# A decoder layer on one core: scores two batches behind, heads inside the loop, two single last batches

## The reference, cut to what matters

```
# 1. attention, 16 heads of 8 channels
q_in = x @ Wq.T + b ; Q = [q_in, conv3(q_in)] @ qproj.T + b      (K the same way, V = x @ Wv.T + b)
tau   = sigmoid(conv1(gelu(dwconv3(x))))                         one value per head and query
delta = sigmoid(conv1(gelu(dwconv3(x))))                         one value per head and key
scores = (Q K^T / sqrt(8)) * tau + delta ; attn = softmax(scores) ; out = attn V @ out_w.T + b
# 2. cross part (mLSTM form), 4 heads of 32 channels, q from the result, k and v from ctx
i, f gates ; log_D = lower triangle of (cumulated log f differences + i) ; D = exp(log_D - rowmax)
C = (q k^T / sqrt(32)) * D ; h = C / max(|sum C|, exp(-rowmax)) @ v ; head norm, times (1 + ln_weight)
# 3. linear with x and weight rounded to a 6 bit grid in blocks of 32, plus bias
```

## Time and profile before

| | us |
|---|---|
| runs | 257.17, 258.87, 253.48 |
| median | 257.17 |
| profiled execution, its own time | 257.06 |
| its span, first to last instruction | 255.2 |
| TensorE busy | 197.6 |
| VectorE busy | 157.1 |
| ScalarE busy | 122.8 |
| GpSimd busy | 130.3 |

### The profile page before, as it was taken

The page is one execution under the profiler, slowest core; times in us unless marked ns, Lnnn a source line. Parts: engine busy times, 40 slices in busy tenths (PEclk is TensorE's granted clock), DMA queues, the critical chain, the costliest instruction groups (busy, mean ns, idle before and its releaser), DMA issues. The chain is left out here.

```text
span 255.2 us, 6255 instructions
## 1 busy us (share of the span) xinstructions
PE 197.6 (77%) x2279; PEld 135.3 (53%) x2279; DVE 157.1 (62%) x383; ACT 122.8 (48%) x333; POOL 130.3 (51%) x246
## 2 busy tenths in 40 slices
...
PEclk9999869899999999799985999989999999555555
...
GB/s 182 147 185 1 3 0 1 1 0 3 3 0 3 85 0 3 85 0 4 3 85 3 0 105 3 0 106 1 6 100 6 3 103 23 2 85 0 21 21 21
DMA packets 11454, 8.94 MB, mean 35 GB/s; under 512 B 2745, under 2 KB 10401, under 8 KB 11425
## 3 DMA queue, kind: packets, MB, share of 16 engines
...
HBM read 7.47 MB, written 1.08 MB: 34 GB/s over the span
## 5 line engine op out<-in xcount | busy, mean ns | idle before, releaser
L1005 DVE TENSOR_REDUCE nm<-score 128x8 f32<-128x1024 f32 x32 | 39.0, 1222 | 24.1 <-PE score L604 24.0
L501 ACT ACTIVATE u<-score 128x1024 f32<-128x1024 f32 x32 | 32.6, 1018 | 27.7 <-PE score L616 27.7
L604 PE MATMUL score<-km,qf 32*128 32x512 f32 x128 | 36.2, 662 | 5.0 <-ACT u L501 3.0
L610 PE MATMUL score<-qm,kf 32*128 32x512 f32 x128 | 37.0, 652 | 0.0
L813 PE MATMUL bankPV<-u,vz 128*32 128x128 f32 x512 | 18.6, 290 | 6.5 <-ACT u L501 6.5
L286 POOL TENSOR_SCALAR qm<-qf,mcol 128x512 f32<-128x512 f32 x16 | 11.7, 749 | 23.0 <-DVE qf L993 16.9
L616 PEld LDWEIGHTS score<-nmT,sel 32*128 32x128 bf16 x256 | 10.9, 95 | 18.0 <-issue 18.0
L863 PE MATMUL bankY<-ctm,xt 128*128 128x33 f32 x128 | 18.4, 303 | 2.0 <-ACT y1s L515 0.6
L813 PEld LDWEIGHTS bankPV<-u,vz 128*32 128x32 f32 x512 | 14.0, 114 | 10.4 <-ACT u L501 8.6
L863 PEld LDWEIGHTS bankY<-ctm,xt 128*128 128x128 f32 x128 | 17.6, 220 | 3.2 <-DVE xt L1070 2.0
L813 PE MATMUL bankPV<-u,ez 128*32 128x128 f32 x512 | 18.7, 291 | 0.0
...
## 6 DMA issues: line engine op xcount, KB each, us to landing
...
```

Source lines behind the costliest of these rows:

```text
L501: nc.scalar.activation(prob[:, i % 2, k:k + 2, :].rearrange("p k s -> p (k s)"), sc[:, 512 * k:512 * (k + 2)], ACT.Exp, scale=SQ_SCALE).th ...
L604: ins = mm(sc[:, 512 * k:512 * (k + 1)], qf[r, n, :], km[r, n % (2 * CB)].rearrange("p j s -> p (j s)"), start=True, stop=True)
L610: mm(sc[:, 512 * k:512 * (k + 1)], kf[r, n, :], qm[r, n % (2 * CB)].rearrange("p j s -> p (j s)"), start=True, stop=False)
L1005: nc.vector.tensor_reduce(nm[:, i % 2, J * k:J * (k + 2)], sc[:, 512 * k:512 * (k + 2)].rearrange("p (h s) -> p h s", s=S), AX_X, ALU.max, ...
```

## The change

- `GR` replaces the eight pairs by nine groups: seven pairs, then batches 14 and 15 alone. Every step of the rest takes its width from it.
- Scores: `v1.i` and `v2.i` now hold a(i) and b(i-2). Two new steps `aa.0`, `aa.1` hold a(0), a(1) alone, `bb.14`, `bb.15` hold b(14), b(15) alone. `nm`, `nmx` and `nmT` get three buffers instead of two.
- Heads: `u` has two chunks instead of four, so the middle tap of chunk 2 or 3 waits until `tau` or `del` two chunks before is done. In the lists the taps 6 and 7, their gelus, `tau.2`, `tau.3`, `del.3` and their tanh stand inside the loop. For them ScalarE loads the gelu set again (`gelu.1`) and then the exp set again (`exp.1`). exp(delta) and its transpose are made by chunk. `diag` and the unused convolution step are gone. ctx chunks 2 and 3 are loaded once `cT.0`, `cT.1` have freed their buffers.
- Groups 7 and 8 (`BY_ROWS`): `dec` no longer reads the spread gates. A new TensorE step `ld` writes a bf16 mask into bank P and adds each gate row by a matmul with one column of the identity, repeated over all partitions; `dec` takes four exponentials with the other gate as bias. `spread` is not issued for them, nor `dm`.
- The step `hl` (GpSimd) multiplies by (1 + ln_weight) right after `hs`; `z2` and the centring inside `qa` are VectorE's. `hc` and `zc` are gone, `zb` follows `qa`, and `z2`, `z2c`, `z2b`, `z3` share one buffer `z`.
- `y1s` has five buffers instead of three. In `y1` the residual's matmul comes first.

```diff
+GR = ((0, 2), (2, 2), (4, 2), (6, 2), (8, 2), (10, 2), (12, 2), (14, 1), (15, 1))
+BY_ROWS = (7, 8)
+YR = 5
-TAU_BANK = ("S2", "S3", "PV", "PV")
+TAU_BANK = ("S2", "P", "P", "P")
+DEL_BANK = ("Y", "P", "P", "P")
 PE_ORDER = """
+    tx.0 ab.0 hw.0 mT.0 mT.1 wT.0 tx.1 del.0 tx.2 wT.1 tau.0 K.0 del.1 Q.0 Q.1 tx.3 del.2 aa.0 Q.2 gw.0 aa.1 tau.1 cg.0 nmT.0 ow.0 v1.2 nmT.1 K.1 edT.0
+    v2.2 edT.1 K.2 v1.3 V.0 edT.2 rc.0 v2.3 nmT.2 cT.0 pv.0 cm.0 v1.4 cm.1 pv.1 nmT.3 v2.4 V.1 y1.0 v1.5 nmT.4 tau.2 v2.5 gF.0 pv.2 v1.6 nmT.5 pv.3 tau.3
+    yT.0 del.3 MT.0 K.3 v2.6 edT.3 y1.1 V.2 v1.7 nmT.6 V.3 pv.4 qk.0 gF.1 V.4 v2.7 hst.0 v1.8 MT.1 pv.5 nmT.7 v2.8 cT.1 yT.1 v1.9 cT.2 pv.6 dT.0 v2.9
...
+    v1.15 nmT.14 pv.12 v2.15 y1.5 cm.7 pv.13 nmT.15 bb.14 dT.3 cm.8 y1.6 gF.5 qk.4 ffn.3 MT.5 pv.14 yT.5 bb.15 gF.6 hst.4 qk.5 MT.6 y1.7 yT.6 pv.15 hst.5
+    yT.7 qk.6 y1.8 gF.7 dT.4 ld.7 ffn.4 gF.8 qk.7 hst.6 dT.5 ld.8 ffn.5 MT.7 hst.7 yT.8 MT.8 qk.8 dT.6 ffn.6 hst.8 dT.7 ffn.7 dT.8 ffn.8
 DVE_ORDER = """
+    cent.0 sel.0 ab.0 tapT.0 tapD.0 hw.0 mT.0 tapD.1 mT.1 tapT.1 wT.0 bias.0 tapD.2 tapT.2 tapD.3 tapT.3 wT.1 tapT.4 bias.1 kf.0 tapD.4 qf.0 tapD.5 qs.0
+    qf.1 tapT.5 wd.0 mY.0 mX.0 qf.2 gw.0 mX.1 mY.1 cg.0 qs.1 tapD.6 mX.2 tapD.7 ow.0 kf.1 tapT.6 mY.2 tapT.7 kf.2 mX.3 vz.0 rc.0 mY.3 gc.0 mX.4 gc.1 att.0
...
+    z2.4 gb.7 bn.4 att.8 qa.4 lf.7 nrm.5 zb.4 vs.5 scan.7 cc.6 gb.8 z2.5 lf.8 bn.5 z3.4 qa.5 scan.8 zb.5 cc.7 nrm.6 vs.6 z2.6 z3.5 bn.6 dd.7 qa.6 nrm.7
+    dd.8 vs.7 zb.6 cc.8 z2.7 bn.7 z3.6 qa.7 zb.7 nrm.8 vs.8 z3.7 z2.8 bn.8 qa.8 zb.8 z3.8
 ACT_ORDER = """
+    xT.0 geT.0 geD.0 geD.1 xT.1 thD.0 geT.1 xT.2 geD.2 thT.0 geT.2 geD.3 geT.3 thD.1 geT.4 geD.4 geD.5 xT.3 thD.2 geT.5 thT.1 nmT.0 exp.0 edx.0 edx.1
+    edx.2 eY.0 nmT.1 edc.0 eX.0 edc.1 eY.1 edc.2 eX.1 cT.0 nmT.2 cm.0 eY.2 cm.1 rec.0 nmT.3 eX.2 y1s.0 sq1.0 nmT.4 eY.3 l1.0 eX.3 gelu.1 geT.6 geD.6 geT.7
+    thT.2 nmT.5 geD.7 thT.3 yT.0 thD.3 exp.1 eY.4 edx.3 em.0 rec.1 dec.0 eX.4 edc.3 y1s.1 sq1.1 eY.5 nmT.6 l1.1 eX.5 hs.0 hq.0 eY.6 em.1 rh.0 rec.2 nmT.7
...
 SP_ORDER = """
+    ctx.2 spread.0 spread.1 ctx.3 store.0 spread.2 spread.3 store.1 spread.4 store.2 spread.5 store.3 spread.6 store.4 store.5 store.6 store.7 store.8
...
+                    if c >= 2:
+                        pool.wait_ge((tau_ps, del_ps)[n], c - 1)
...
+                elif name == "hl":
...
+                    nc.gpsimd.tensor_tensor(hsl[:, i % 2, 0:NH * nb].rearrange("p (h v) d -> p h v d", v=nb),
+                                            hs[:, i % 2, 0:NH * nb].rearrange("p (h v) d -> p h v d", v=nb)[:, :, :, 0:DH],
+                                            rows[:, 0, :].rearrange("p (h d) -> p h d", h=NH).unsqueeze(2).to_broadcast([P, NH, nb, DH]),
+                                            ALU.mult).then_inc(hl_done, 1)
...
+                elif name == "gelu":
+                    nc.scalar.preload_act_table_set("gelu_and_others")
+                elif name == "exp":
+                    nc.scalar.preload_act_table_set("natural_log_exp_and_others")
...
+                    for h in range(NH):
+                        ins = nc.scalar.activation(dec[:, i % 2, S * h:S * (h + 1)], pb[:, S * h:S * (h + 1)], ACT.Exp, bias=g[:, i % 2, h:h + 1])
...
                 elif name == "v1":
...
+                    score_a(i, (0, 1), aX)
...
+                    score_b(i - 2, (2, 3))
+                    pe.wait_ge(nmT_sb, i - 1)
+                    less_max(i - 2, (2, 3), bY)
...
+                elif name == "ld":
+                    free("P")
+                    mm(pb[:], identb[:], maskb[:].unsqueeze(1).to_broadcast([P, NH, S]), start=True, stop=False)
+                    pe.wait_ge(nG_done, i + 1)
+                    for h in range(NH):
+                        ins = mm(pb[:, S * h:S * (h + 1)], ident[0:NH, h:h + 1].to_broadcast([NH, P]), nG[0:NH, i % 2, :], start=False, stop=(h == NH - 1))
...
+                elif name == "z2":
...
+                    dve.wait_ge(hl_done, i + 1)
+                    link(nc.vector.tensor_tensor(hc[:, i % 2, 0:nb].rearrange("p v h d -> p h v d"),
+                                                 hsl[:, i % 2, 0:w].rearrange("p (h v) d -> p h v d", v=nb),
+                                                 hn8[:, 5, 0:w].rearrange("p (h v) -> p h v", v=nb).unsqueeze(3).to_broadcast([P, NH, nb, DH]),
+                                                 ALU.mult))
...
+                    nc.vector.tensor_tensor(z[:, i % 2, 0:nb], hc[:, i % 2, 0:nb].rearrange("p v h d -> p v (h d)"), x1[:, i % 2, 0:nb],
+                                            ALU.add).then_inc(z2_done, 1)
...
                 elif name == "qa":
...
+                    for v in range(nb):
+                        ins = nc.vector.tensor_scalar(z[:, i % 2, v, :], z[:, i % 2, v, :], mv[:, i % 2, v, 0:1], None, ALU.subtract)
```

More of the change, by code:

```diff
@@ L31 @@
 J = 4
-PAIRS = B // 2
 VS = 40
@@ L40 @@
 LN_1E6 = -13.815510557964274
+GR = ((0, 2), (2, 2), (4, 2), (6, 2), (8, 2), (10, 2), (12, 2), (14, 1), (15, 1))
+NG = len(GR)
+GROUP_OF = {b0 + v: (p, v) for p, (b0, nb) in enumerate(GR) for v in range(nb)}
+BY_ROWS = (7, 8)
+YR = 5
 K_BANK = ("S0", "P", "P", "P")
 Q_BANK = ("S1", "P", "P", "P")
-TAU_BANK = ("S2", "S3", "PV", "PV")
-CONV_CHUNKS = ()
-CONV_BANK = ()
+TAU_BANK = ("S2", "P", "P", "P")
+DEL_BANK = ("Y", "P", "P", "P")
 PE_ORDER = """
[L50 to L56, removed]
@@ L73 @@
[L73 to L76, removed]
@@ L230, in load_c @@
             def load_c(c):
-                load(cin[:, c], ctx[CB * c:CB * (c + 1)].rearrange("b s d -> s b d"), c_in[c])
+                load(cin[:, c % 2], ctx[CB * c:CB * (c + 1)].rearrange("b s d -> s b d"), c_in[c])
             load(pk[:], kproj_w, w_p)
@@ L255, in _ @@
                 load(rows[:, i, :], v.partition_broadcast(P), w_r)
-            for c in range(1, NC):
-                load_c(c)
+            load_c(1)
             for name, i in steps(SP_ORDER):
-                if name == "spread":
+                if name == "ctx":
+                    sp.wait_ge(cT_ps, i - 1)
+                    load_c(i)
+                elif name == "spread":
+                    b0, nb = GR[i]
+                    w = NH * nb
                     sp.wait_ge(nG_done, i + 1)
-                    sp.dma_start(scr[i:i + 1, :].rearrange("o (h s) -> (o h) s", s=S), nG[:, i % 2, :]).then_inc(nG_out, 16)
+                    sp.dma_start(scr[i:i + 1, 0:w * S].rearrange("o (h s) -> (o h) s", s=S), nG[0:w, i % 2, :]).then_inc(nG_out, 16)
                     sp.wait_ge(nG_out, 16 * (i + 1))
```

632 lines of the change are left out of this document (327 added, 305 removed).

## The result

The changed kernel takes 238.57 us (median; 237.39 to 240.98 in the first four runs), beside 258.02 us for the kernel before on the same chip. The ratio is 0.933, 95% interval 0.916 to 0.950. In a second set of six runs it took 237.81 us, ratio 0.929 [0.924, 0.934]. The forecast was 235 us. An execution more than 1.5% above the fastest of its own kernel is left out of every comparison here, and where that changes a figure, the executions that count are named. The profiled execution is the one of 237.39 us, with a span of 235.7.

A forecast was written before the change was run, and what follows sets the result against it. The prediction saw three limits: VectorE's queue in the head, TensorE's work in the middle, latency in the tail. pv.15 at 193 plus a tail of 40.3 gave a 233.3 us span, with 1.9 outside it 235 us; range 224 to 249.

The forecast's parts named there:

- Part 1: Head: VectorE loses diag and four tap pairs ahead of the first maximum, which starts at about 40.5 us instead of 47.97.
- Part 2: Ramp: taps return between the maxima; v1.4 starts near 65 us, with about 5 us of idle TensorE before it.
- lent head: Rival: head's gain lost in the ramp, tail saves nothing: 250 us, with surviving waits 255, centre 253; chance 0.13.
- Part 3: Loop from v1.4: TensorE's work 118.8 us, idle 6, clock loss 3.4, so pv.15 starts at 193.
- Part 4: Second table load: ScalarE's block of 7.9 us, covered by 8.0 us of TensorE's steps, costs 0 to 1 us.
- Part 5: Tail from pv.15 to the end: 40.3 us instead of 48.2, bounds 36 and 48.
- Term (a): Tail: last group's gates by matmuls instead of through DRAM take 2.8 us instead of 11.3, -8.5 us.
- Step (d): Tail: batch 14 as its own group puts about 6 us of VectorE's steps between those of batch 15, +6 us.
- (b) to (e): Tail: hst for one batch -1.8, steps after hst -6.1, batch 14's own group +6, nine groups' hand-overs +2.5 us.
- waits survive: Rival: in the loop the new fillers end as the old did, idle 12 us, clock dips as before: 245 us; chance 0.14.
- table not covered: Rival: a late tap makes ScalarE's block of 7.9 us stand in TensorE's way: 243 us; chance 0.08.
- clock down in the ramp: Rival: TensorE, busy little more than half the time from aa.0 to v1.4, stays at 1.2 GHz: 265 us; chance 0.07.

The follow-up runs named there:

- run 8: Changed kernel with all taps, gelus, tanhs, tau and del ahead of the loop and one table load, in two TensorE orders: 251.38 us, then 253.13 us.
- run 10: Changed kernel with pv of batches 1 to 12 up to half a round earlier on TensorE's queue: 252.12 us, ratio to before 0.978.
- run 9: Changed kernel with one more load each of the exponential and gelu tables in ScalarE's block: 241.33 us; 238.64 and 239.95 count.
- run 6: Changed kernel with the gates of the two single batches through DRAM, one-hot and mask matmuls gone: 241.97 us; 238.46 and 240.37 count.
- run 1: Changed kernel with 104 extra matmuls nobody reads, before the steps on which TensorE waits after pv.15: 234.01 us, ratio to before 0.915.
- run 7: Changed kernel with batches 14 and 15 as one pair again, gates through DRAM: 251.45 us; only 246.93 counts.

## Why the prediction held, step by step

**Part 1** (first maximum at 40.5): 40.30. Right to 0.2 us. GpSimd's taps are not always ahead of VectorE's, as I had assumed; one wait of 1.12 us falls into the ramp.

**Part 2** (`v1.4` at 65): 65.06, by luck in part, since two errors cancel. `v1.2` starts at 46.99, not 44; TensorE idles 1.7 us from there, not 5. VectorE is not without gaps as forecast (21.3 of 24.8 us busy). In the orders of run 8 moving the taps back makes the ramp no shorter. The rival of the lent head is refuted for the two orders tried.

**Part 3** (work 118.8, idle 6, clock 3.4, `pv.15` at 193): busy 119.4, idle 5.8, clock 0, `pv.15` at 190.26. The work and the idle time hold; the clock loss is the mis-sized term, 3.4 for 0. That other work between an exponential and the next writer of its bank keeps the idle time away is borne out by run 10: the scores stay two batches behind, only `pv` moves, and 12 us of idle time come back. So the lag alone does not keep it away; whether the same places for `pv` could be had with a lag of one batch, no run tries. Nor do the dips of the clock follow from idle time, as the forecast took them to: run 10 idles 17.7 us at a clock of 1.00, and the loop of run 8, with 7.5 us, has a dip. Why they are gone stays open.

**Part 4** (0 to 1 us of waits): 1.1 us in TensorE's two steps, within the idle time above. The block is 10.0 us long, not 7.9; 2.2 of these ScalarE spends waiting for `tau.3`'s matmuls. Run 9 puts the slack at 0.9 us, so the forecast was right with less room than a free load would need. The Trainium skill, page "ScalarE: Activation LUTs", section "Rules for kernel authors", asks to finish one table set before switching; here the order that switches is the faster one, by 15 us against run 8, where more than the tables differs. Its 2.7 us a switch did not show: in run 9 each load takes 1.28 us and the next activation starts 1.30 us after the last load began.

**Part 5** (tail 40.3, bounds 36 and 48): 45.4, 5.1 us more. Here the terms were mis-sized. Term (a) put the new way of the gates at 2.8 us from the sums to the product, instead of 11.3. It takes 7.9 us for batch 14 and 12.6 for batch 15. Mask, gate sums and exponentials are 0.63 + 2.07 + 1.14 = 3.8 of it, the rest is standing in queues, so the last group gained nothing on this stretch. Against DRAM the new way is worth 1.3 us (run 6), not 8.5. Step (d) counted 6 us of VectorE's work for batch 14's own group and nothing for TensorE, whose work in the tail rose from 21.95 us to 29.44, nearly all of it at half clock. Holding the clock gives 4.5 us back (run 1). That is close to the 5.1 missed, but it is not the same quantity: the forecast started from a tail whose clock was 0.61 too, and how much of the 7.5 us of added matmuls lies in the chain, no run shows. What (b) to (e) are worth one by one stays open, since the pair of run 7 was queued badly.

**Sum.** Forecast 235, measured 238.6: +5.1 in the tail, -2.7 ahead of it, and the rest the distance of the profiled execution from the median. The range 224 to 249 held it, helped by errors of opposite sign. Of the rivals, "waits survive" (245), "table not covered" (243) and "clock down in the ramp" (265) did not happen; of the last a trace exists, one slice of half clock in some executions, worth 2.8 us. The reason given for this last one was wrong: from the first maximum to `v1.4` TensorE is busy 21.3 of 24.8 us, not little more than half the time. And the 255 us given for the lent head with the surviving waits do not add up: 250 + 6 + 3.6 is 260.
